# One of a quad's four down tiles ahead of the fourth product, three behind the third

## What is computed

```
x = x.reshape(-1, H)                                   # 2048 x 512, layer-normalized
scores = softmax(x @ gate_w.T)                         # 64 experts
topk_w, topk_idx = top_k(scores, 8)
flat = w_e[:, inv_map]; scalar = flat.sum(-1)          # 8 groups of 8
soft = softmax(where(flat == 0, -1e9, flat))
xg = x[:, None, :] + einsum('ngi,ghi->ngh', soft, mask_up_w)
g, u = einsum('ngh,gih->ngi', xg, gate_proj_w), einsum('ngh,gih->ngi', xg, up_proj_w)
d = einsum('ngi,ghi->ngh', silu(g) * u, down_proj_w)   # inner width 352
y = einsum('ng,ngh->nh', scalar, d)                    # added, scaled, to the input
```

## Time and profile before

| | us |
|---|---|
| median of 3 runs | 1077.0 (1076.57 to 1082.37) |
| the profiled execution | 1075.6 |
| its span, first to last instruction | 1073.8 |
| TensorE busy | 1051.0 |
| VectorE busy | 745.3 |
| GpSimd busy | 610.7 |
| ScalarE busy | 387.6 |

### The profile page before, as it was taken

One profiled execution on the slowest core, in us unless ns is written; L12 is line 12 of the kernel. 1 busy time (PEld: TensorE's weight loads), 2 busy tenths in 40 slices (PEclk: granted clock), 3 DMA queues, 4 the chain that ended last, 5 costly groups with the idle time before them and its releaser, 6 DMA issues.

```text
span 1073.8 us, 14516 instructions
## 1 busy us (share of the span) xinstructions
PE 1051.0 (98%) x5388; PEld 890.7 (83%) x5388; DVE 745.3 (69%) x1336; ACT 387.6 (36%) x651; POOL 610.7 (57%) x531
## 2 busy tenths in 40 slices
PE   8999999999999899999999999999999999999998
PEld 8888988988988688888877788888888888888886
DVE  7774665676667787787779888765675665666655
ACT  5233324334342444334324332333333333332331
POOL 1211102132433857777778888767677777668661
PEclk9999999999999999999999999999999999999999
DMA  9212225255786341215234433393311212221202
GB/s 330 73 40 99 60 49 145 63 128 148 234 241 193 105 52 54 74 40 72 86 113 40 130 126 103 125 335 115 113 54 66 74 39 64 73 73 48 74 27 79
DMA packets 114134, 111.65 MB, mean 104 GB/s; under 512 B 20880, under 2 KB 96400, under 8 KB 114064
## 3 DMA queue, kind: packets, MB, share of 16 engines
q1 hardware_dynamic: 113696, 110.58, 35.8%
q10 hardware_dynamic: 368, 0.15, 0.1%
HBM read 79.05 MB, written 31.65 MB: 103 GB/s over the span
## 4 chain that ended last, share of the span: by engine, by line
PE 83%; DVE 10%; ACT 2%; issue 2%; SPq 1%; DMA 1%; POOL 0%; DVEq 0%; ACTq 0%
PE bank L76 44%; PE bank L1635 31%; PE bank L1641 4%; PE bank L1466 2%; DVE a_stack L1315 1%; SPq L474 1%; PE bank L1649 1%; DVE tmp L1324 1%; DVE a_stack L1313 1%; DVE tmp L1438 1%; DVE xres L1331 1%; DMA soft_stacks<-soft_out 1%; DVE tmp L1427 1%; DVE a_tmp L1307 1%; ACT tmp L1001 0%
## 5 line engine op out<-in xcount | busy, mean ns | idle before, releaser
L1635 PE MATMUL bank<-x2t,wgu_hi 128*128 128x512 f32 x1144 | 353.0, 390 | 0.0
L650 POOL TENSOR_TENSOR wgu_lo<-wgu_raw,wgu_hi 128x512 fp32r<-128x512 f32 (+1 forms) x129 | 210.5, 1638 | 90.1 <-ACT wgu_hi L797 88.4
L1635 PEld LDWEIGHTS bank<-x2t,wgu_hi 128*128 128x128 f32 x1144 | 214.9, 188 | 44.2
L1635 PE MATMUL bank<-x2t,wgu_lo 128*128 128x512 f32 x572 | 224.6, 393 | 3.4 <-DVE tmp L1375 2.5
L797 ACT CAST wgu_hi<-wgu_raw 128x512 fp32r<-128x512 f32 (+1 forms) x129 | 93.7, 726 | 224.6 <-PE bank L1641 188.4
L1331 DVE TENSOR_TENSOR xres<-xres,bank 128x512 f32<-128x512 f32 x176 | 120.0, 682 | 53.6 <-PE bank L76 53.3
L76 PE MATMUL bank<-wd_hi,at_second 128*128 128x512 f32 x336 | 130.8, 389 | 0.0
L1635 PEld LDWEIGHTS bank<-x2t,wgu_lo 128*128 128x128 f32 x572 | 107.4, 188 | 27.9 <-issue 3.5
L624 POOL TENSOR_TENSOR kt_lo<-ctxt_raw,kt_hi 128x256 fp32r<-128x256 f32 x32 | 23.0, 748 | 144.1 <-ACT kt_hi L822 144.1
L1324 DVE TENSOR_TENSOR tmp<-tmp,scalars 128x512 f32<-128x512 f32 x88 | 99.2, 1127 | 3.0
L76 PE MATMUL bank<-wd_hi,at_first 128*128 128x512 f32 x256 | 99.8, 390 | 0.0
(11 more groups left out here) (216 smaller groups left out, 2255.8 us busy)
## 6 DMA issues: line engine op xcount, KB each, us to landing
wgu_raw<-in_w_gate_up SPq DMA_DIRECT2D x43, 512.0 KB, 4.1
wd_raw<-in_w_down SPq DMA_DIRECT2D x22, 512.0 KB, 5.1
a_stacks<-a_stack SPq DMA_DIRECT2D x22, 192.0 KB, 1.9
a_stack<-a_stacks SPq DMA_DIRECT2D x22, 192.0 KB, 4.0
ctxt_raw<-in_ctx_t SPq DMA_DIRECT2D x8, 512.0 KB, 10.9
ctx_raw<-in_ctx SPq DMA_DIRECT2D x8, 512.0 KB, 7.5
x<-x_raw SPq DMA_DIRECT2D x8, 512.0 KB, 7.9
sums_raw<-x SPq DMA_DIRECT2D x16, 256.0 KB, 3.7
```

The lines of the kernel that those rows point to most:

```text
L650: nc.gpsimd.tensor_tensor(wgu_lo[:, group], raw_of(quad)[:, group], f32(wgu_hi[:, group]), ALU.subtract).then_inc(s_fw_lo, 1)
L1635: last = nc.tensor.matmul(out_bank[:], stationary, moving, start=begins and n == 0, stop=n == len(pairs) - 1, skip_group_check=True)
```

## The change

early_tiles gives 1 instead of 2 for quads 3 to 42. On TensorE tile 0 alone stands between soft_products and product_4; tile 1 moves behind product_3, ahead of tiles 2 and 3. The waits that guarded tile 1 in some quads move with it. On VectorE, which uses the same function, one add_down stands ahead of the routing steps and c21, and tiles 1 and 2 are added behind c12. Quads 0, 1, 2 and 43 stay as they are.

```
 def early_tiles(q):
 
-    return 0 if q <= 2 or q == QUADS - 1 else 2
+    return 0 if q <= 2 or q == QUADS - 1 else 1
...
                 soft_products(quad)
                 for n in range(early):
+                    down(below + n)
+                product_4(quad)
+                product_3(quad)
+                for n in range(early, 4):
                     if n == 1 and q == 4:
                         pe.wait_ge(s_centre, B)
                     if n == 1 and q in (5, 9):
...
                         pe.wait_ge(s_flat_sb, B - 1 if q == 6 else B)
                     if n == 1 and q in (8, 13, 18):
                         pe.wait_ge(s_st_sb, {8: B - 2, 13: B - 1, 18: B}[q])
-                    down(below + n)
-                product_4(quad)
-                product_3(quad)
-                for n in range(early, 4):
                     if q == 2 and n == 0:
                         pe.wait_ge(s_logit_sb, B)
                     if q == 2 and n == 1:
```

## The result

| | before | changed |
|---|---|---|
| median | 1078.68 us (4 runs, 1076.57 to 1082.37) | 1098.08 us (4 runs, 1095.57 to 1099.46) |
| the profiled execution | 1075.6 | 1095.57 |
| its span | 1073.8 | 1093.8 |

The changed kernel is slower: the ratio is 1.0165, 95% interval 1.0136 to 1.0194, so +15 to +21 us. The forecast was 1092.0, in a range of 1081 to 1100. Its +15.0 stood on 1077.0, the median of three runs of the kernel before; the fourth run raised that to 1078.68, which is 1.7 of the 6.1 us between forecast and measurement.

The account below looks back on a forecast made before the run. TensorE's own work was taken to bound the kernel. Late tiles 11.6 plus GpSimd's interference 8.4, less 5.0 returned, gave +15.0 us on the profiled 1075.6, so 1090.6; with 1.4 to the median, 1092.0, range 1081 to 1100.

Parts of the forecast that it names:

- +15.0: Feed-forward stage, net loss in us: 20.0 for late last tiles in routing quads, less 5.0 of earlier waits coming back.

Follow-up runs that it names:

- e1: The change made in quads 3 to 18 alone, with quads 19 to 42 left as in the kernel before: 1096.05 us against 1079.47, ratio 1.0147.

## What to carry to other kernels

A tile that waits for the buffer of the tile before last is bound to where another engine drains that one: when tiles are moved on one engine, write down for each the drain that it waits for and what stands ahead of that drain. When TensorE is full, 0.2 us of margin in a steady beat is enough, and where a release comes late in a few quads the lateness is paid in full, with about 0.3 us on top for each wait. Between VectorE and GpSimd, move work into a stretch where the other does not hold a long operation: the same routing steps cost 6.5 us less in the changed kernel, and gained 2.7 us in the kernel before, for an earlier place.

## What was not expected of the hardware

Behind some long waits of TensorE the granted clock fell to 1.2 GHz for 3.4 us. The profiled executions of the changed kernel and the experiments have 22 waits of 1.8 us or more behind quad 2; it happened within about 2 us of the end of 12 of them, once behind a wait of 1.83 us, and nowhere else in the stage. In each of the 12 the stretch lasts 3.4 us, with TensorE busy in nearly all of it, so 1.7 us are missing. Behind the waits of 2.74 us (quad 3) and 2.12 us (quad 14) of the changed kernel it did not happen. In e1 two such stretches follow waits of 2.75 us:

```profile
394.00:402.00 8.00, 6.38 (x23) 5.19 (x24) 4.43 (x8) 2.97 (x6) 0.04 (x1) 0.79 0.70 40
598.00:606.00 8.00, 5.71 (x18) 4.62 (x19) 4.81 (x7) 2.33 (x4) 3.45 (x3) 0.79 1.12 29
```

A mean of 0.79 over 8 us is 1.7 us missing. What picks one wait and not the other isn't settled here.
